# A later block's seventh mask one pair of tiles sooner, the weights' low parts in other heads, GELU's table loaded behind the last exponential

## The chip, the cores and the metric

The kernel runs on one core of one Trainium2 chip. The metric is the device time of one execution in microseconds (us); less is better.

## The reference

One layer of attention over a graph with 2048 nodes, 256 features and 8 heads of 32, in float32. The source side is normed twice (a layer norm and a rectifier, then the layer's own norm), the target side once. Logits are masked by an adjacency matrix of integers before the softmax. Projection, second norm, a feed-forward part with 1024 hidden features and sums follow.

```python
h = maximum(layernorm(x), 0)
hs, ht = layer_norm(h, g1, b1), layer_norm(h_target, g1, b1)
q = (ht @ Wq + bq).reshape(T, 8, 32) / sqrt(32)
k, v = (hs @ Wk + bk), (hs @ Wv + bv)            # in heads
logits = where(adj != 0, einsum('thd,shd->hts', q, k), -1e30)
ctx = einsum('hts,shd->thd', softmax(logits), v).reshape(T, 256)
ht = layer_norm(ht + ctx @ Wo + bo, g2, b2)
out = x + ht + gelu(ht @ W1) @ W2                # tanh form of gelu
```

## The kernel before

**Tiling.** The targets are cut into 4 blocks of 512. A unit is one block and one head, so there are 32 units; unit u has block k = u // 8 and place r = u % 8 in the block. A unit has 16 steps, one for each tile of 128 sources, and 8 pair indices j, one for two steps.

**One step.** TensorE makes the scores of step n + 5 in one of two banks (`scores`: four products that put in the mask and one of keys and queries), ScalarE takes the exponential of them into one of 8 slots of `prob` (`exponential`, L945), and the float32 result is used as two 16-bit parts: the high one is read in place, the low one is a subtraction (`low_part`). VectorE makes the low parts of the steps in `DVE_LO` (2, 6, 10 and 14 of most units, L1324), GpSimd the other twelve (L1532). TensorE then multiplies both parts with the values (`context`). At the end of a unit ScalarE reads the context (`context_out`, L967).

**Row maxima.** The exponential needs a shift for each row. TensorE therefore makes the scores of a unit already some 14 pairs ahead, as `early` products of 128 targets by 1024 sources, in two banks of two halves each, one half in each step. VectorE subtracts the mask and takes the maximum of each (`maxima`, L1316). The early product e waits for the maxima of e - 2, as it writes the same bank. In unit u, pair index j handles e = 8u + 14 + j.

**Masks.** For the next block the adjacency of 512 by 2048 is loaded in eight pieces of 128 by 1024 (512 KB each) into two buffers `adj_in`, and turned into a mask. ScalarE makes pieces 0 and 7, VectorE pieces 1 to 6 at the places (r, j) of `MASK_DVE` (`make_mask`, L1304). In VectorE's program one pair index has this order:

```python
            if k + 1 < NTB and (r, s - 3) in QP_AT:
                query_low(k + 1, QP_AT[r, s - 3])
        for n in lo_here(u, j):
            low_part(n)
        for e in pairs_at(u, j):
            maxima(e)
        ...
        if k + 1 < NTB and (r, j) in MASK_DVE:
            make_mask(k + 1, MASK_DVE[r, j])
```

SyncE issues all loads and copies in one queue: for a block the pieces of the mask, at r = 4 the last two of them, then the 12 copies of the next block's queries (`place_q`) behind the query low part.

**Other work in the loop**, at fixed places (r, s): transposes of targets, queries and contexts on TensorE through one bank `aux`, norms on ScalarE, statistics (`lead_stats` at r = 3, j = 3 to 6) on VectorE, low parts of features on GpSimd. At (4, 1) of blocks 1 to 3 ScalarE takes a square root and so loads a table and, for the next exponential, loads another.

**Weights.** `W1` and `W2` are also used in two 16-bit parts. ScalarE makes the eight high parts at s = 6 of the units in `HIGH_AT` = 3, 4, 5, 6, 7, 12, 13, 14 (`weight_high`), GpSimd the eight low parts (`weight_low`, L1578) behind step 12 of the units in `LOW_AT`. All are read after the loop, but for the first four low parts, on which the normed features of block 0 wait in unit 29.

**After the loop** come the feed-forward products: `up_products` in groups of 6 matmuls, `gelus` on ScalarE (L1189), then the high part (L1193), the low part on VectorE, `down_products`. A product of index f waits for the GELU of f - 2.

The engines run their programs in order; waits are semaphores, and each change of order is one of the program text. Table loads of ScalarE are put by the compiler ahead of the first activation that needs another table.

Of the kernel before, what the change touches and what calls it, by code (L numbers as in the profile page):

```python
# [10 lines left out]
ACT = mybir.ActivationFunctionType  # L11
# [51 lines left out]
HT_AT = {(5, 1): 0, (5, 4): 1}  # L63


MASK_DVE = {(2, 3): 1, (2, 6): 2, (3, 2): 3, (3, 7): 4, (4, 3): 5, (4, 7): 6}


MASK_ACT = {0: [(0, 2), (0, 4), (0, 11), (0, 13)], 7: [(5, 13), (5, 15), (6, 1), (6, 3)]}
# [22 lines left out]


HIGH_AT = [3, 4, 5, 6, 7, 12, 13, 14]
LOW_AT = [4, 5, 6, 7, 13, 14, 15, 21]


DVE_LO = [(10, 14)] + [(4, 9, 14) if u == UNITS - 3 else (2, 6, 10, 14) for u in range(1, UNITS - 2)] + [tuple(range(1, STEPS, 2))] * 2
# [2 lines left out]
def head_of(r):  # L101

    return r % 2 * TT + r // 2
# [71 lines left out]
def masks_dve(k, i):  # L175

    return min(i + 1, FIRST_DVE) if k == 0 else len(MASK_DVE) * (k - 1) + FIRST_DVE + min(i, len(MASK_DVE))

# [16 lines left out]
def gnn_kernel(nc, x, adj, nodemask, h_target, ln1_scale, ln1_bias, Wq, bq, Wk, bk, Wv, bv, Wo, bo,  # L195
               ln2_scale, ln2_bias, W1, W2, out):
    with ExitStack() as top:
# [6 lines left out]
        def sem(name):  # L204
            return top.enter_context(nc.semaphore(name))
# [49 lines left out]
        big_c, eps_c, warm_c = (big[:, i:i + 1] for i in range(3))  # L255
# [58 lines left out]
        dve_link, act_link, pool_link = sem("dve_link"), sem("act_link"), sem("pool_link")  # L314
# [62 lines left out]
        def raw_of(k):  # L377
            return raw[:, k % 2, :].rearrange("p (t h w) -> p t h w", t=TT, h=H)
# [21 lines left out]
        with nc.Block() as block:  # L400
# [464 lines left out]
            def _(act):  # L865
# [7 lines left out]
                def affine(dst, tile, scale, bias):  # L873
                    return nc.scalar.activation(dst, tile, ACT.Identity, bias=bias, scale=scale)
# [62 lines left out]
                def exponential(n):  # L937
                    act.wait_ge(score_ready, n + 1)
                    if n >= SLOTS:
                        act.wait_ge(ctx_done, n - SLOTS + 1)  # L940
                    elif n == 0:

                        act.wait_ge(mask_dve, FIRST_DVE)
                        act.wait_ge(mask_pool, PAIRS - FIRST_DVE)
                    nc.scalar.activation(prob[:, n % SLOTS, :], score[n % 2][:, :], ACT.Exp).then_inc(exp_done, 1)  # L945
# [14 lines left out]
                def row_out(u):  # L960
                    job_here("shift", u)
                    nc.scalar.activation(q_block(u // H)[SHIFT_ROW:SHIFT_ROW + 1, u % H, :], aux[SHIFT_ROW:SHIFT_ROW + 1, :],
                                         ACT.Copy).then_inc(aux_done, 1)

                def context_out(u):
                    act.wait_ge(ctx_done, (u + 1) * STEPS)
                    nc.scalar.activation(raw_of(u // H)[:, :, head_of(u % H), :], ctx_v, ACT.Copy).then_inc(ctx_out, 1)  # L967
# [107 lines left out]
                def normed_high(k, c, bank):  # L1075
                    if k > 0:

                        act.wait_ge(h_lo, DC * (k - 1) + c + 1)
                    else:
                        act.wait_ge(w_lo, 4)  # L1080
                    read, count = (h_done, DC * (k - 1) + c + 1) if k > 0 else (aux_done, AUX["hT", 0, c] + 1)
                    affine(h_full[:, c, :], bank, LN2_G[:, c:c + 1], LN2_B[:, c:c + 1]).then_inc(read, 1)
                    act.wait_ge(read, count)
                    nc.scalar.activation(h_bufs[k % 2][:, 0, c, :], h_full[:, c, :], ACT.Copy).then_inc(h_hi, 1)
# [44 lines left out]
                for u in range(UNITS):  # L1129
                    k, r = divmod(u, H)  # L1130
                    for s in range(STEPS):
                        n = u * STEPS + s
                        if s == 0 and u > 0:
                            context_out(u - 1)
                        if n + AHEAD < TILES:
                            exponential(n + AHEAD)
                        job = aux_job(u, s + 2)
                        if job == ("shift", u + 1):
                            negated(u + 1)
                        if aux_job(u, s - 1) == ("shift", u + 1):  # L1140
                            row_out(u + 1)
                        if k == 0 and (r, s) in T_HIGH[0]:
                            feature_high(0, T_HIGH[0].index((r, s)))
                        if k + 1 < NTB and (r, s) in T_HIGH[1]:
                            feature_high(k + 1, T_HIGH[1].index((r, s)))
                        if (u, s) == WO_HIGH:
                            output_high()
                        if s == 6 and u in HIGH_AT:
                            weight_high(HIGH_AT.index(u))
                        if k + 1 < NTB:  # L1150
                            if act_mask_at(k, r, s):
                                i, part = act_mask_at(k, r, s)
                                mask_part(k + 1, i, part)
                            if r == 2 and s in TARGET_STEPS:
                                target_norm(k + 1, TARGET_STEPS.index(s))
                            if (r, s - 1) in QT_AT:
                                query_features(k + 1, QT_AT[r, s - 1])
                            if (r, s - 2) in QP_AT:
                                if QP_AT[r, s - 2] == 0:
                                    for g in range(TT):  # L1160
                                        act.wait_ge(q_placed[g], PLACE * (k + 1))
                                query_high(k + 1, QP_AT[r, s - 2])
                        if k > 0:
                            for part in range(NORM_STEPS):
                                if (r, s - part) in NORM_AT:
                                    context_norm(k - 1, NORM_AT.index((r, s - part)), part)
                            if (r, s - 1) in CT_AT:
                                context_T(k - 1, CT_AT[r, s - 1])
                            if (r, s - 2) in CT_AT:
                                context_high(k - 1, CT_AT[r, s - 2])  # L1170
                            if (r, s - 2) in WO_AT:
                                rows_out(k - 1, WO_AT[r, s - 2])
                            if r == 4 and s == 1:
                                row_deviation(k - 1, lead_width(k - 1))
                            if r == 5 and s in (2, 4, 7, 11):
                                second_norm(k - 1, (2, 4, 7, 11).index(s))
                        if k == NTB - 1:
                            if (r, s - 1) in HT_AT:
                                job_here("hT", 0, HT_AT[r, s - 1])
                                normed_high(0, HT_AT[r, s - 1], aux[:, :])  # L1180
                context_out(UNITS - 1)


# [40 lines left out]
            def _(dve):  # L1224
# [207 lines left out]
                for u in range(UNITS):  # L1432
                    k, r = divmod(u, H)
                    for j in range(PAIRS):
# [9 lines left out]
                        if u == 0 and j in (4, 5):  # L1444
                            target_norm(j - 3)
                        if k + 1 < NTB and (r, j) in MASK_DVE:
                            make_mask(k + 1, MASK_DVE[r, j])
                        if k > 0:
# [73 lines left out]
            def _(pool):  # L1522
# [51 lines left out]
                def weight_low(i):  # L1574
                    pool.wait_ge(w_hi, i + 1)
                    lo, w, hi = (a.rearrange("p c n -> p (c n)")[:, i % 4 * TB:(i % 4 + 1) * TB]
                                 for a in ((w1_lo, w1, w1_hi) if i < 4 else (w2_lo, w2, w2_hi)))
                    nc.gpsimd.tensor_tensor(lo, w, hi, ALU.subtract).then_inc(w_lo, 1)  # L1578
# [44 lines left out]
                for u in range(UNITS):  # L1623
                    k, r = divmod(u, H)
                    for m in range(STEPS):
                        if m not in DVE_LO[u]:
                            low_part(u * STEPS + m)
                        if k > 0 and (r, m) == LEAD_SCALE:
                            lead_scale(k - 1, lead_width(k - 1))
                        if k > 0 and (r, m) in SUM_AT:  # L1630
                            context_sum(k - 1, SUM_AT.index((r, m)))
                        if k == 0 and (r, m) in T_LOW[0]:
                            feature_low(0, T_LOW[0].index((r, m)))
                        if k + 1 < NTB and (r, m) in T_LOW[1]:
                            feature_low(k + 1, T_LOW[1].index((r, m)))
                        if k > 0 and (r, m) in C_LOW:
                            context_low(k - 1, C_LOW.index((r, m)))
                        if (u, m) == WO_LOW:
                            output_low()
                        if m == 12 and u in LOW_AT:  # L1640
                            weight_low(LOW_AT.index(u))

                for t in range(TT):
                    context_sum(NTB - 1, t)
# [39 lines left out]
```

## Time and profile before

| | us |
|---|---|
| median of 3 runs | 683.53 |
| the runs | 681.89, 683.53, 683.69 |
| the profiled execution's own time | 682.28 |
| its span | 680.3 |
| TensorE busy | 649.9 |
| VectorE busy | 567.2 |
| GpSimd busy | 542.4 |
| ScalarE busy | 501.5 |

The span runs from the first to the last instruction in the profile. Matmuls are pipelined and their ends are modelled: one of 512 columns has a duration of 0.38 us, and the next one starts 0.22 us behind its start. So idle time of TensorE under about 0.15 us doesn't show as such. The granted clock of TensorE was 1.00 in every stage of the loop. The names in the rows are those of the tensors; where two share memory, the older name may stand (`nTq`, `qT` and `kT` in the rows of the feed-forward part, `w_f` for the 16-bit weights).

### The profile page before, as it was taken

What the parts mean: (1) busy time and instruction counts of PE and PEld (TensorE: products, weight loads), DVE (VectorE), ACT (ScalarE), POOL (GpSimd) and SP (SyncE); (2) the same over time, 40 slices, a digit from 0 to 9 for tenths busy, and PEclk for the clock granted to TensorE, in tenths of its full rate; (3) what the DMA queues carried; (4) which work ended last, traced back from release to release, by engine and by line L of the source; (5) the groups of instructions that cost most, each with busy time, mean ns of one, the idle gap of its engine ahead of it and who ended that gap; (6) DMA issues with size and microseconds to landing.
All of it is one profiled execution on the core that took longest, in us unless ns stands there. A gap on an engine that the chain in (4) does not pass through costs nothing. (4 is left out here: it accounts for less than half of the span.)

```text
span 680.3 us, 20543 instructions
## 1 busy us (share of the span) xinstructions
PE 649.9 (96%) x8402; PEld 464.2 (68%) x8402; DVE 567.2 (83%) x940; ACT 501.5 (74%) x973; POOL 542.4 (80%) x508
## 2 busy tenths in 40 slices
PE   4999999999999999999999999999999999899998
PEld 4556677766777777677777766777777667457767
DVE  5989899999989979888988798899878887595561
ACT  4767687777789858787898686877976788877450
POOL 4565889999999967999999679999997777383430
PEclk9999999999999999999999999999999999999999
DMA  8835512212101011220011112011000000000001
GB/s 290 281 91 151 167 33 64 64 50 63 33 2 34 2 65 63 67 76 2 2 33 33 64 55 57 19 67 59 4 2 1 2 2 2 1 1 32 24 18 54
DMA packets 20797, 36.23 MB, mean 53 GB/s; under 512 B 2752, under 2 KB 13280, under 8 KB 20704
## 3 DMA queue, kind: packets, MB, share of 16 engines
q1 hardware_dynamic: 20704, 34.92, 16.5%
q8 instruction: 66, 1.08, 0.7%
q14 instruction: 27, 0.22, 0.1%
HBM read 26.49 MB, written 2.10 MB: 42 GB/s over the span
## 5 line engine op out<-in xcount | busy, mean ns | idle before, releaser
L1532 POOL TENSOR_TENSOR prob_lo<-prob 128x512 f16<-128x512 f32 x379 | 432.5, 1168 | 45.7 <-ACT prob L945 44.7
L945 ACT ACTIVATE prob<-score 128x512 f32<-128x512 f32 x512 | 303.8, 597 | 110.4 <-PE score L514 102.5
L514 PE MATMUL score<-nidentb,mask_nat 128*128 128x128 bf16 x2048 | 198.3, 219 | 4.2 <-ACT prob L945 1.6
L514 PEld LDWEIGHTS ctx<-v_sb,prob 128*128 128x128 bf16 x2048 | 158.8, 98 | 61.9 <-ACT raw L967 13.8
L514 PE MATMUL early<-kT,qT 96*128 96x512 f16 x512 | 191.8, 380 | 6.7 <-DVE half_max L1316 5.7
L514 PE MATMUL score<-qT,kT 97*128 97x512 f16 x512 | 195.3, 381 | 0.0
L514 PE MATMUL ctx<-v_sb,prob 128*128 128x65 f16 x2048 | 191.5, 193 | 2.9 <-ACT raw L967 2.5
L1316 DVE CUSTOM_DVE_ANT_0 early<-early,mask_nat,half_max 128x1024 f32<-128x1024 f32 x128 | 163.9, 1286 | 33.3 <-PE early L514 31.7
L514 PE MATMUL ctx<-v_sb,prob_lo 128*128 128x65 f16 x2048 | 190.4, 193 | 0.0
L514 PEld LDWEIGHTS ctx<-v_sb,prob_lo 128*128 128x128 f16 x2048 | 142.6, 97 | 49.7 <-issue 4.0
L1316 DVE CUSTOM_DVE_ANT_0 early<-early,mask_nat 128x1024 f32<-128x1024 f32 x128 | 157.0, 1229 | 19.3 <-PE early L514 16.6
L1324 DVE TENSOR_TENSOR prob_lo<-prob 128x512 f16<-128x512 f32 x133 | 133.7, 1006 | 4.1 <-ACT prob L945 4.0
L514 PEld LDWEIGHTS score<-nidentb,mask_nat 128*128 128x128 bf16 x2048 | 121.5, 97 | 9.9 <-ACT prob L945 4.3
L514 PEld LDWEIGHTS early<-kT,qT 96*128 96x128 f16 x512 | 50.3, 99 | 17.5 <-DVE half_max L1316 13.3
L514 PEld LDWEIGHTS score<-qT,kT 97*128 97x128 f16 x512 | 50.1, 98 | 0.0
L514 PE MATMUL early<-w_f,kT 128*128 128x256 f16 x384 | 42.8, 273 | 1.1 <-DVE adj_in L1484 1.1
L1461 DVE TENSOR_TENSOR kT<-qT,kT 128x512 f16<-128x512 f32 x32 | 28.0, 885 | 17.7 <-ACT kT L1193 17.5
L514 PEld LDWEIGHTS early<-w_f,kT 128*128 128x128 f16 x384 | 37.4, 98 | 6.6 <-DVE adj_in L1484 1.7
L1660 POOL TENSOR_TENSOR mask_nat<-mask_nat,tgt 128x256 f32<-128x256 f32 x16 | 16.5, 1039 | 27.4 <-DVE mask_nat L1475 27.4
L1316 DVE DVE_READ_ACCUMULATOR2_ANT half_max<- 128x1 f32 x256 | 35.4, 138 | 0.0
L1189 ACT ACTIVATE qT<-score 128x512 f32<-128x512 f32 x32 | 19.0, 592 | 17.0 <-PE score L514 12.2
L983 ACT ACTIVATE q_stage<-raw,rden 128x32 f32<-128x32 f32 x96 | 25.3, 316 | 0.2
(185 smaller groups left out, 650.7 us busy)
## 6 DMA issues: line engine op xcount, KB each, us to landing
adj_in<-in_adj SPq DMA_DIRECT2D x26, 512.0 KB, 3.9
qT<-q_stage SPq DMA_DIRECT2D x48, 64.0 KB, 2.0
kT<-mask_nat SPq DMA_DIRECT2D x48, 64.0 KB, 2.0
raw<-in_x SPq DMA_DIRECT2D x4, 512.0 KB, 5.4
tgt<-in_L_gnn_h_target SPq DMA_DIRECT2D x4, 512.0 KB, 11.3
prob<-in_adj SPq DMA_DIRECT2D x4, 512.0 KB, 10.1
nT<-in_L_gnn_W SPq DMA_DIRECT2D x2, 1024.0 KB, 6.2
mask_nat<-in_x SPq DMA_DIRECT2D x1, 2048.0 KB, 9.7
```

What stands on the lines that cost most here:

```text
L514: return nc.tensor.matmul(dst, w, m, start=start, stop=stop, **more)
L945: nc.scalar.activation(prob[:, n % SLOTS, :], score[n % 2][:, :], ACT.Exp).then_inc(exp_done, 1)
L983: last = nc.scalar.activation(cnorm[:, t, h * HD:(h + 1) * HD], raw_of(k)[:, t, h, 0:HD], ACT.Copy, scale=rden[:, t * H + h:t * H + h + 1])
L1189: nc.scalar.activation(gelu[:, f % 2, :], up[f % 2][:, :], ACT.Gelu_apprx_tanh).then_inc(gelu_ready, 1)
L1316: nc.vector.tensor_tensor_reduce(out=early[e % 2][:, :], in0=early[e % 2][:, :], in1=mask_nat[:, k % 2, t, half * HALF:(half + 1) * HALF], ...
L1324: nc.vector.tensor_tensor(prob_lo[:, n % SLOTS, :], prob[:, n % SLOTS, :], prob_hi(n % SLOTS), ALU.subtract).then_inc(lo_sem["dve"], 1)
L1461: nc.vector.tensor_tensor(g_lo[:, k % 2, f, :], gelu[:, f % 2, :], g_hi[:, k % 2, f, :], ALU.subtract).then_inc(g_lo_done, 1)
L1532: nc.gpsimd.tensor_tensor(prob_lo[:, n % SLOTS, :], prob[:, n % SLOTS, :], prob_hi(n % SLOTS), ALU.subtract).then_inc(lo_sem["pool"], 1)
L1660: nc.gpsimd.tensor_tensor(xin[:, n - 1, :], xin[:, n - 1, :], tgt[:, n - 1, :], ALU.add).then_inc(r_done, 1)
```

## The change

Three edits. The seventh mask (piece 6) of the blocks 1 to 3 is made at pair index 6 of the unit with r = 4, where it was index 7. The eight low parts of weights stand behind other steps: three in unit 11, three in unit 19 and two in unit 20, where it was one each in eight units. And ScalarE runs a one-column GELU on a constant behind the loop and ahead of the last `context_out`, so that the table is loaded there.

```diff
-MASK_DVE = {(2, 3): 1, (2, 6): 2, (3, 2): 3, (3, 7): 4, (4, 3): 5, (4, 7): 6}
+MASK_DVE = {(2, 3): 1, (2, 6): 2, (3, 2): 3, (3, 7): 4, (4, 3): 5, (4, 6): 6}
...
-LOW_AT = [4, 5, 6, 7, 13, 14, 15, 21]
+LOW_AT = [(11, 3), (11, 8), (11, 13), (19, 3), (19, 8), (19, 13), (20, 2), (20, 7)]
...
+
+                nc.scalar.activation(warm_c, eps_c, ACT.Gelu_apprx_tanh).then_inc(act_link, 1)
                 context_out(UNITS - 1)
...
-                        if m == 12 and u in LOW_AT:
-                            weight_low(LOW_AT.index(u))
+                        if (u, m) in LOW_AT:
+                            weight_low(LOW_AT.index((u, m)))
```

## Rows read from the trace of the kernel before

**Rows 1.** The page, part 1: busy us, share of the span, instructions.

```profile
PE 649.9 (96%) x8402; PEld 464.2 (68%) x8402; DVE 567.2 (83%) x940; ACT 501.5 (74%) x973; POOL 542.4 (80%) x508
```

**Rows 2.** The waits of TensorE, 90 to 575 us: total, times, longest.

```profile
PE early L514 <- DVE half_max L1316: 4.3, 9, 0.9
```

**Rows 3.** Windows of three units: length, then busy us (instructions) of each engine.

```profile
149.06:165.34 16.28, 15.57 (x230) 10.74 (x229) 15.78 (x23) 11.85 (x22) 16.28 (x14) 1.00 0.31 83
165.34:180.40 15.06, 14.89 (x229) 10.91 (x229) 12.65 (x20) 12.02 (x23) 15.06 (x15) 1.00 0.12 37
245.38:263.07 17.69, 17.51 (x257) 13.50 (x257) 14.40 (x29) 12.08 (x23) 12.92 (x13) 1.00 0.17 54
```

**Rows 4.** The lines of two operations: duration in ns, least/median/most.

```profile
L1304 DVE TENSOR_SCALAR mask_nat<-adj_in x20: 676/825/1504, 33.8 to 414.9; 128x1024 bf16<-128x1024 int32 x20
...
L1324 DVE TENSOR_TENSOR prob_lo<-prob x133: 677/954/1566, 74.1 to 580.1; 128x512 f16<-128x512 f32 x133
...
L1532 POOL TENSOR_TENSOR prob_lo<-prob x379: 1031/1040/1577, 63.8 to 579.4; 128x512 f16<-128x512 f32 x190
```

**Rows 5.** The page, part 6: one kind of DMA issue, us to landing.

```profile
adj_in<-in_adj SPq DMA_DIRECT2D x26, 512.0 KB, 3.9
```

**Rows 6.** VectorE in order of time: start, duration, [idle before].

```profile
146.60 1.29 DVE L1316 CUSTOM_DVE_ANT_0 early<-early,mask_nat,half_max 128x1024 f32<-128x1024 f32 x1 [0.78 <-PE early L514]
...
148.47 0.71 DVE L1324 TENSOR_TENSOR prob_lo<-prob 128x512 f16<-128x512 f32 x1
149.10 1.28 DVE L1316 CUSTOM_DVE_ANT_0 early<-early,mask_nat,half_max 128x1024 f32<-128x1024 f32 x1
...
150.31 1.32 DVE L1304 TENSOR_SCALAR mask_nat<-adj_in 128x1024 bf16<-128x1024 int32 x1
...
154.00 1.28 DVE L1316 CUSTOM_DVE_ANT_0 early<-early,mask_nat,half_max 128x1024 f32<-128x1024 f32 x1
```

**Rows 7.** TensorE in order of time, two early matmuls.

```profile
150.83 0.38 PE L514 MATMUL early<-kT,qT 96*128 96x512 f16 x1
...
155.39 0.39 PE L514 MATMUL early<-kT,qT 96*128 96x512 f16 x1 [0.47 <-DVE half_max L1316]
```

**Rows 8.** GpSimd in order of time, the first low part of the weights.

```profile
142.91 1.16 POOL L1578 TENSOR_TENSOR w_f<-nT,w_f 128x512 f16<-128x512 f32 x1
```

**Rows 9.** VectorE in order of time, unit 11.

```profile
253.33 0.69 DVE L1304 TENSOR_SCALAR mask_nat<-adj_in 128x1024 bf16<-128x1024 int32 x1
...
258.84 0.76 DVE L1324 TENSOR_TENSOR prob_lo<-prob 128x512 f16<-128x512 f32 x1
259.51 1.22 DVE L1316 CUSTOM_DVE_ANT_0 early<-early,mask_nat 128x1024 f32<-128x1024 f32 x1
```

**Rows 10.** GpSimd in order of time, unit 11 and, last, unit 20.

```profile
250.69 2.04 POOL L1532 TENSOR_TENSOR prob_lo<-prob 128x512 f16<-128x512 f32 x2 [0.74 <-ACT prob L945]
...
258.00 3.48 POOL L1532 TENSOR_TENSOR prob_lo<-prob 128x512 f16<-128x512 f32 x3 [0.64 <-ACT prob L945]
...
399.97 3.04 POOL L1532 TENSOR_TENSOR prob_lo<-prob 128x512 f16<-128x512 f32 x3 [2.85 <-ACT prob L945]
```

**Rows 11.** TensorE in order of time, one early matmul.

```profile
260.96 0.38 PE L514 MATMUL early<-kT,qT 96*128 96x512 f16 x1
```

**Rows 12.** ScalarE in order of time, at the end of the attention.

```profile
573.28 6.76 ACT L945 ACTIVATE prob<-score 128x512 f32<-128x512 f32 x10 [0.43 <-PE score L514]
581.94 0.39 ACT L967 ACTIVATE raw<-ctx 128x260 f32<-128x260 f32 x1 [1.90 <-PE ctx L514]
582.35 1.28 ACT L1189 ACT_TABLE_LOAD   x1
583.64 0.60 ACT L1189 ACTIVATE qT<-score 128x512 f32<-128x512 f32 x1
...
588.00 0.60 ACT L1189 ACTIVATE qT<-score 128x512 f32<-128x512 f32 x1 [0.79 <-PE score L514]
```

**Rows 13.** TensorE in order of time, the first up products.

```profile
581.74 4.05 PE L514 MATMUL score<-nTq,w_f 128*128 128x512 f16 x18
```

## The prediction

> **What bounds the kernel now.** I read the page first: TensorE is busy 649.9 of 680.3 us and the other three engines 501.5 to 567.2 [rows 1]. So a change pays only where TensorE stands still or is held up, and it costs only where it makes TensorE stand. Then I read who makes TensorE wait between 90 and 575 us, the attention loop without its fill: the longest entry is 4.3 us in nine waits for the row maxima of VectorE (`half_max`, L1316) [rows 2]. The other entries name ScalarE, none names GpSimd. Then I read the windows of single units (one head of one target block, 16 steps). An undisturbed unit takes 15.06 us; the unit behind the one whose end carries the seventh mask (149.06 to 165.34, the sixth unit of the first block) takes 16.28, though it has no more matmuls (230 against 229) [rows 3]. This 1.2 us is the stall that the first edit is near to, and the same pattern comes once in each of the three blocks that have a next one. GpSimd is busy for the whole of these two units, but for only 12.92 of 17.69 us of the first unit that gets new work [rows 3].
>
> One more view carries the argument: how long one and the same instruction takes. A low part on VectorE takes 677 to 1566 ns, a mask 676 to 1504 ns, a low part on GpSimd 1031 to 1577 ns [rows 4]. The shapes are equal. In the order of time the short VectorE durations stand where GpSimd is idle or just between two instructions, the long ones where a GpSimd instruction has just begun. So an instruction of VectorE with both ends in SBUF waits for the running one of GpSimd, up to 1566 - 677 = 0.89 us, and GpSimd's next one pays about half a microsecond (up to 1577 ns for 1040). The maxima (1.22 to 1.29 us) read PSUM and stay put. Work that moves on GpSimd therefore has a price on VectorE, and VectorE is what TensorE waits for. The Trainium skill has this as a rule ("SBUF — State Buffer", the diagram's notes: the pair of ports that VectorE and GpSimd share is an exclusive lock, held for a whole instruction, and the other one blocks fully). The trace agrees in direction; its longest delay of VectorE, 0.89, is under the 1.04 us of one GpSimd instruction that the rule allows, and by the rule the upper bounds below would each be 0.15 higher.
>
> **The mask a pair sooner.** The seventh mask of blocks 1 to 3 goes from behind `maxima` of pair index 7 of the fifth unit to behind that of index 6. Counts and waits are unchanged, as it is still the sixth of its block on VectorE. Its input was loaded into `adj_in` when the fifth mask was made, about a unit earlier, and lands in 3.9 us [rows 5], so no new wait. In the first block VectorE is idle for 0.78 us before the maxima at 146.60 and from there without a gap until behind 155 us [rows 6]. The mask stays behind those maxima, so it doesn't go into the gap. What was maxima, query low part, low part, maxima, mask, maxima becomes maxima, mask, query low part, low part, maxima, maxima: the same instructions, the same sum, the same end. What changes is what lies between: the second of these maxima (149.10 + 1.28 = 150.38) ends about 1.24 us later (1.32 less the overlap of neighbours), at 151.6. The early matmul that needs it ran at 150.83 [rows 7]: a new stall of about 151.7 - 150.8 = 0.9 us. The matmul at 155.39 waited for the maxima that end at 154.00 + 1.28 = 155.28 [rows 6, 7], which don't move, so the old stalls behind (0.47 of idle at 155.39 [rows 7] and smaller ones that the modelled ends of matmuls hide; 1.2 in all by the units' lengths) shrink by as much as the new one costs. Net 0 in each of three blocks. The low part for step 2 of the next unit (148.47 + 0.71 = 149.18 [rows 6]) ends some 1.3 us later, about 150.5, and its context product comes at about 151.1 or later: hidden. The query low part also ends 1.3 us later, and with it SyncE issues 12 copies of queries (`place_q`); their first reader is more than a unit later, so hidden, and the next block's first load behind them in the same queue has a whole unit too. Bound: the mask and the low part land on another phase of GpSimd, at worst 0.8 us either way, per block; three draws together, plus or minus 1.0. I take 0.
>
> **The weights' low parts.** Eight instructions of GpSimd of 1.16 us [rows 8], in units 4, 5, 6, 7, 13, 14, 15, 21 before, are now three each in units 11 and 19 and two in unit 20 (counted from 0). Their inputs, the high parts, are made in units 3 to 14 and each stands ahead of its low part; their readers (the normed features of unit 29 and the products after the loop) come later. Units 11 and 19 have r = 3: GpSimd has 17.69 - 12.92 = 4.8 us free there, 3 x 1.16 = 3.5 fits [rows 3]. The context products don't wait for it.
>
> But where it fits in, it meets VectorE. In unit 11 GpSimd works off two low parts at 250.69 to 252.73, VectorE's mask at 253.33 runs behind them in 0.69 us, and before 258.00 it is idle for 0.64, so VectorE's low part at 258.84 takes 0.76 [rows 9, 10]. The new instruction behind step 8 moves the second of the pair to about 252.8 to 253.8: the mask waits some 0.3 us more. The one behind step 13 ends at about 258.7, the low part of step 15 then runs to about 259.7, and VectorE's low part, begun at 259.1, ends at about 260.3 in place of 259.6: 0.7 us later in all. The maxima behind it end at 259.51 + 1.22 = 260.73 now [rows 9], and 261.43 then; the early matmul that reads them came at 260.96 [rows 11]. A waiting matmul starts 0.11 behind the end of its maxima (155.39 against 155.28 [rows 6, 7]), so TensorE stands 261.43 + 0.11 - 260.96 = 0.57 us. It is not given back: the next point at which VectorE holds TensorE lies behind idle time of VectorE, so it starts from TensorE's own delay. Unit 19 has the same order: 0.57 again. Bounds for each: 0 if the phases miss, and 2 x 0.89 - 0.12 = 1.7 if both instructions pay in full.
>
> Unit 20 has ScalarE's two table loads, in which GpSimd is idle for 2.85 us [rows 10]; the first of its two new instructions, 1.16 us, shifts work into that idle time, in which VectorE now has a mask and a low part for itself, at the short end of their durations [rows 4]; the second pushes the rest of the unit by 1.15. VectorE has about a microsecond there before TensorE asks, half of it just won by the stall of unit 19. I take +0.2, between 0 and 0.9.
>
> What the eight leave: GpSimd's run behind the first, from 144.07 on [rows 8], starts 1.15 us sooner. It frees no wait that TensorE has today [rows 2], only other phases for the two shared instructions that end in the stall of unit 5. I take -0.3, between -1.2 (the whole stall) and +0.5. In units 6, 7, 13 to 15 and 21 nothing waits: 0.
>
> **GELU's table.** Today the load of 1.28 us starts at 582.35 behind `context_out`, and the first GELU runs at 583.64; the change loads it behind the last exponential (573.28 + 6.76 = 580.04), in the 1.90 us in which ScalarE waits for the last context product: 580.05 to 581.33, and the small activation 0.2, so 0.4 before 581.94 [rows 12]. Free. The gain is none as well: TensorE runs the first three groups of the up projection as 18 matmuls in one piece of 4.05 us from 581.74 and is not held by the first GELU; by 588.00 ScalarE itself has waited 0.79 us for TensorE, and everything behind hangs on that point [rows 12, 13]. 0; if the cover were gone, `context_out` would be late by at most the 1.28, and even that comes back in the first GELU. The Trainium skill ("ScalarE: Activation LUTs", What ACT_TABLE_LOAD costs) gives 1283 ns and a drain of about 1380 more for a switch. The load is 1.28 here, but the activation follows at once (582.35 + 1.28 = 583.63 against 583.64). By the page `context_out` would be about 1.0 late and the sum still unchanged.
>
> **Sum.** 2 x 0.57 + 0.2 - 0.3 + 0 + 0 = +1.0 us. On the profiled execution's own 682.28 us (its span is 680.3, with 2.0 around it) that is 683.3; that execution lies 1.25 below the median of the runs, 683.53, so the forecast for the median is 684.5.
>
> **Rivals.**
> (1) All is hidden: the new instructions meet VectorE in other phases than today's rows say, about 0. For it: only the 0.23 us between 260.73 and 260.96 decide, and they are read off one execution. Against it: GpSimd's order fixes the phase. 683.5.
> (2) The mask's move does dissolve the stall of unit 5, 13 and 21: up to 1.2 us in each, 3.6 in all, 679.9. This needs VectorE to have idle time ahead of the mask's new place that it lacks at the old one, or GpSimd to stand still there. Against it: no gap on VectorE from 146.60 to 155. Half of it, 1.8, would be 681.7.
> (3) The load of GELU's table was on the path: 1.3 less, 682.2. Against it: the unbroken 18 matmuls.
> (4) Slower: VectorE pays in full for GpSimd's new work. At 1.7 in unit 11 and in unit 19 and 0.9 in unit 20 it is 4.3 less 0.3, 687.5; it passes 0.3% when the mask and the low part in units 11 and 19 lose together 1.0 or more each, against 0.7 in my working. For it: GpSimd's new instructions stand where it is idle today [rows 10].
>
> **How the numbers follow.** A measurement of this kernel can tell about 0.3% (2.05 us) from no change. Chances: my forecast (+0.3 to +2.0) 0.50; (1) 0.27; (2) 0.08, of which half passes 0.3%; (3) 0.04; (4) 0.11. Faster by over 0.3%: 0.05; within: 0.84; slower: 0.11. The range 682.0 to 686.3 takes in (1), (3) nearly, the near half of (4) and the spread of the three runs (1.8 us); the rest of (2) and (4) is outside.
>
> **What would show it.** After: the mask row directly behind the maxima of index 6, an early matmul in step 2 of units 5, 13 and 21 that waits 0.8 to 0.9 us for `half_max`, and less waiting in steps 4 and 6; those units still about 16.3 us long. In units 11 and 19 the mask near 1.0 and the low part of step 14 near 1.1 us, with an early matmul waiting about 0.5 at the unit's end, and the two units with their followers about 0.6 us longer than now. ScalarE: table load at 580.05, first GELU about 0.4 earlier, the fourth unchanged against TensorE. I am wrong if units 5, 13 and 21 get shorter by 0.5 or more each, or if VectorE's instructions in unit 11 keep 0.69 and 0.76.

## The result, and the profile after

The changed kernel takes 684.07 us (median of 14 runs, 683.83 to 685.64) against 682.03 (median of 14 runs, 681.77 to 683.69): 2.04 us more. The ratio is 1.0031, with a 95% interval of 1.0024 to 1.0038, so it is slower, by about the 0.3% that the prediction took as the least that can be told from no change. The time lies in the range on record; the forecast of +1.0 us was half of what came.

The page of the changed kernel; the span is 2.2 us longer, and no engine has more to do than before but ScalarE, with its one added activation [rows 1].

```profile
span 682.5 us, 20544 instructions
...
PE 649.2 (95%) x8402; PEld 463.0 (68%) x8402; DVE 566.0 (83%) x940; ACT 501.8 (74%) x974; POOL 540.5 (79%) x508
```

The waits of TensorE in its attention loop, 90 to 575 us. The maxima now cost 5.9 us in nine waits, where it was 4.3 [rows 2], and GpSimd has its first entry in this list:

```profile
PE early L514 <- DVE half_max L1318: 5.9, 9, 1.1
...
PE ctx L514 <- POOL prob_lo L1534: 0.2, 1, 0.2
```

Windows of units 5, 6 and 11 (length, busy us of TensorE, its weight loads, VectorE, ScalarE, GpSimd). A unit u is taken from the start of the exponential of step 16u + 5 to that of the next unit. Unit 5 has hardly changed [rows 3]; unit 11 takes 18.42 us for 17.69:

```profile
149.12:165.45 16.33, 15.24 (x230) 10.90 (x229) 15.00 (x24) 11.75 (x23) 14.71 (x13) 1.00 0.31 83
165.45:180.51 15.06, 14.89 (x229) 10.91 (x230) 12.17 (x20) 12.02 (x24) 13.44 (x14) 1.00 0.11 37
245.60:264.02 18.42, 17.74 (x257) 13.35 (x258) 15.23 (x28) 12.10 (x24) 16.88 (x16) 1.00 0.16 51
```

Unit 19 is the same as 11. All lengths that changed, from the starts of these exponentials in each trace (us):

| unit | before | changed | mask only | weights only | mask at index 5 | weights at 3, 4, 5 | weights at 3, 4, 13 | weights at 1, 3, 4 | last version |
|---|---|---|---|---|---|---|---|---|---|
| 5 | 16.28 | 16.33 | 16.43 | 17.14 | 15.98 | 16.32 | 16.31 | 16.32 | 15.35 |
| 7 | 14.90 | 15.08 | 14.90 | 15.07 | 14.90 | 15.07 | 15.08 | 15.08 | 14.90 |
| 11 | 17.70 | 18.41 | 17.70 | 18.40 | 17.70 | 18.59 | 18.03 | 17.69 | 17.69 |
| 13 | 16.25 | 16.40 | 16.39 | 16.25 | 15.40 | 16.40 | 16.40 | 16.39 | 15.40 |
| 15 | 14.90 | 15.08 | 14.90 | 15.08 | 14.90 | 15.08 | 15.08 | 15.07 | 14.90 |
| 19 | 17.69 | 18.41 | 17.70 | 18.41 | 17.69 | 18.59 | 18.03 | 18.59 | 17.69 |
| 20 | 18.72 | 18.77 | 18.72 | 18.76 | 18.72 | 18.71 | 18.77 | 18.72 | 18.73 |
| 21 | 16.39 | 16.62 | 16.55 | 16.44 | 15.55 | 16.42 | 16.62 | 16.41 | 15.56 |

The others stay within 0.1 us, but for unit 28 in the profiles of two kernels (last section). In these rows "changed" less "before" adds up to 2.27 us, and units 10 and 16 give back 0.06 and 0.09: 2.12. Two thirds of it, 1.43, are in units 11 and 19.

**Unit 11.** GpSimd, VectorE and TensorE of the changed kernel in order of time, each in a fence of its own:

```profile
251.91 1.16 POOL L1580 TENSOR_TENSOR w_f<-nT,w_f 128x512 f16<-128x512 f32 x1
...
257.93 1.16 POOL L1580 TENSOR_TENSOR w_f<-nT,w_f 128x512 f16<-128x512 f32 x1
```

```profile
253.56 1.07 DVE L1306 TENSOR_SCALAR mask_nat<-adj_in 128x1024 bf16<-128x1024 int32 x1
...
259.44 1.19 DVE L1326 TENSOR_TENSOR prob_lo<-prob 128x512 f16<-128x512 f32 x1
260.56 1.22 DVE L1318 CUSTOM_DVE_ANT_0 early<-early,mask_nat 128x1024 f32<-128x1024 f32 x1
```

```profile
261.89 0.39 PE L514 MATMUL early<-kT,qT 96*128 96x512 f16 x1 [0.35 <-DVE half_max L1318]
```

The answering rows of before are [rows 9 to 11]. The mask, 0.69 us then, waits for GpSimd's low part behind the new instruction at 251.91 and takes 1.07; the low part, 0.76 then, meets GpSimd's low part behind the new instruction at 257.93 and takes 1.19. The maxima end at 260.56 + 1.22 = 261.78, the early matmul that was issued at 260.96 starts at 261.89, 0.11 behind that end, as worked out. (0.22 of its lateness is from further ahead: unit 11 starts at 245.60 for 245.38.)

**Units 4 and 5.** VectorE, and the early matmul of step 2:

```profile
146.66 1.29 DVE L1318 CUSTOM_DVE_ANT_0 early<-early,mask_nat,half_max 128x1024 f32<-128x1024 f32 x1 [0.89 <-PE early L514]
...
147.87 1.26 DVE L1306 TENSOR_SCALAR mask_nat<-adj_in 128x1024 bf16<-128x1024 int32 x1
...
149.71 0.86 DVE L1326 TENSOR_TENSOR prob_lo<-prob 128x512 f16<-128x512 f32 x1
150.50 1.28 DVE L1318 CUSTOM_DVE_ANT_0 early<-early,mask_nat,half_max 128x1024 f32<-128x1024 f32 x1
...
153.94 1.28 DVE L1318 CUSTOM_DVE_ANT_0 early<-early,mask_nat,half_max 128x1024 f32<-128x1024 f32 x1
```

```profile
151.89 0.39 PE L514 MATMUL early<-kT,qT 96*128 96x512 f16 x1 [1.00 <-DVE half_max L1318]
```

The mask stands behind the maxima at 146.66. The maxima that this matmul needs end at 151.78 for 150.38, and TensorE stands 1.00 us; in return the maxima at 153.94 are over in time, and the wait that stood at 155.39 [rows 7] is gone.

**Unit 7,** where GpSimd has less to do than before, is 0.18 us longer. The waits of TensorE's weight loads, 179.51 to 196.59 us (before, no wait for `half_max` stood there); then GpSimd and VectorE in order of time:

```profile
PEld early L514 <- DVE half_max L1318: 0.5, 2, 0.3
```

```profile
182.99 3.48 POOL L1534 TENSOR_TENSOR prob_lo<-prob 128x512 f16<-128x512 f32 x3 [0.24 <-ACT prob L945]
```

```profile
183.18 1.40 DVE L1326 TENSOR_TENSOR prob_lo<-prob 128x512 f16<-128x512 f32 x1
```

Before, the same low part of VectorE took 1.06:

```profile
182.87 1.06 DVE L1324 TENSOR_TENSOR prob_lo<-prob 128x512 f16<-128x512 f32 x1
```

GpSimd has caught up: it waits for the exponential, starts right behind it, and VectorE's low part begins 0.19 us later and takes 0.72 more than the 0.68 that it takes alone. The next one of the unit goes from 0.95 to 1.37 in the same way.

**The end of the attention,** ScalarE:

```profile
582.24 1.28 ACT L1182 ACT_TABLE_LOAD   x1
583.53 0.20 ACT L1182 ACTIVATE big<-big 128x1 f32<-128x1 f32 x1
584.13 0.39 ACT L967 ACTIVATE raw<-ctx 128x260 f32<-128x260 f32 x1 [0.40 <-PE ctx L514]
585.43 0.60 ACT L1191 ACTIVATE qT<-score 128x512 f32<-128x512 f32 x1 [0.91 <-PE score L514]
...
590.19 0.60 ACT L1191 ACTIVATE qT<-score 128x512 f32<-128x512 f32 x1 [0.88 <-PE score L514]
```

The table load is hidden and `context_out` is not late for it: it waited 0.40 us for TensorE. The small activation follows 0.01 us behind the end of the load, so nothing like the later `context_out` that the prediction worked out from a drain is seen. The fourth GELU (590.19) is 2.19 us behind its time of before, 588.00 [rows 12], which is what was lost up to unit 21. Nothing is gained.

### The profile page after: what moved, and what is told of

It reads as the page before. It is cut to its first block and busy times, and to the rows that moved or that the text cites. A ratio compares the mean times of both kernels' runs of the same rounds, so it can differ in the third digit from the quotient of the medians.

```text
span 682.5 us, 20544 instructions
## 1 busy us (share of the span) xinstructions
PE 649.2 (95%) x8402; PEld 463.0 (68%) x8402; DVE 566.0 (83%) x940; ACT 501.8 (74%) x974; POOL 540.5 (79%) x508
## 3 DMA queue, kind: packets, MB, share of 16 engines
q8 instruction: 66, 1.08, 0.6%
## 5 line engine op out<-in xcount | busy, mean ns | idle before, releaser
L1326 DVE TENSOR_TENSOR prob_lo<-prob 128x512 f16<-128x512 f32 x133 | 129.8, 977 | 4.0 <-ACT prob L945 4.0
```

The lines of the kernel that those rows point to most:

```text
L1326: nc.vector.tensor_tensor(prob_lo[:, n % SLOTS, :], prob[:, n % SLOTS, :], prob_hi(n % SLOTS), ALU.subtract).then_inc(lo_sem["dve"], 1)
```

## The experiments

The theories: (A) the loss is VectorE's two-sided SBUF instructions meeting GpSimd's new work in units 11, 19 and 20; (B) it is the new stall of 1 us in units 5, 13 and 21; (D) VectorE's gapless stretch makes the stall of these units, and the mask would fit into the gap ahead of it.

**The three edits one by one,** and the mask one pair further.

```diff
# mask alone: the first hunk of the change; weights alone: the second and the last; GELU alone: the third
# mask at pair index 5, on the kernel before:
-MASK_DVE = {..., (4, 3): 5, (4, 7): 6}
+MASK_DVE = {..., (4, 3): 5, (4, 5): 6}
```

> The kernel before with the mask's edit alone. Theory A (the loss comes from GpSimd's new work in units 11, 19 and 20, which VectorE's instructions wait for; the mask's move only moves a stall): units 5, 13 and 21 within 0.2 us of the kernel before each, the whole +0.1 to +0.5 us (ratio 1.0002 to 1.0007). Rival B (the stall of 1.0 us in step 2 that shows in units 5, 13 and 21 of the changed kernel is the loss): about +1.5 us or more, ratio 1.002 or over.

> The kernel before with the low parts of the weights at their new steps alone. Theory A: +1.5 to +2.0 us, ratio 1.0022 to 1.0029, with units 11 and 19 at 18.4 us for 17.7. Rival B: under +0.7 us.

> The kernel before with the GELU ahead of the last context read alone. Both theories: 0, within 0.2 us. A third, that the table load was on the path, says -1.3 us (ratio 0.998).

> The kernel before with the seventh mask two pairs sooner, at pair index 5 of the fifth unit. Theory D (VectorE's gapless stretch behind the maxima at 146.60 makes the stall of the next unit, and the idle 0.8, 1.8 and 1.7 us ahead of those maxima can hold the mask): the stall of units 5, 13 and 21 goes, these units fall from 16.3 to about 15.3 us, the whole -2 to -3.3 us (ratio 0.995 to 0.997). Rival (the stall is not made by the mask, or the mask there makes the maxima late by as much): 0 within 0.5 us.

| kernel | median us (runs) | before, us | ratio, 95% interval |
|---|---|---|---|
| mask alone | 682.71 (11) | 682.15 | 1.0010, 1.0001 to 1.0018 |
| weights alone | 684.75 (5) | 682.15 | 1.0042, 1.0030 to 1.0055 |
| GELU alone | 682.01 (11) | 682.15 | 1.0001, 0.9992 to 1.0010 |
| mask at index 5 | 680.18 (7) | 682.15 | 0.9974, 0.9963 to 0.9985 |

The mask alone costs 0.56 us, hardly more than the 0.5 that I expected of it at most, the GELU nothing, and the weights 2.6: theory B falls. A is right on units 11 and 19, but too low as a whole (1.5 to 2.0 expected), for it had no loss in unit 5. The edits don't add up: 0.56 + 2.6 - 0.14 = 3.0 against 2.04. The table shows the place: unit 5 takes 17.14 us with the weights alone and 16.33 with the mask moved too. VectorE there, with the weights alone:

```profile
148.30 1.58 DVE L1324 TENSOR_TENSOR prob_lo<-prob 128x512 f16<-128x512 f32 x1
149.81 1.28 DVE L1316 CUSTOM_DVE_ANT_0 early<-early,mask_nat,half_max 128x1024 f32<-128x1024 f32 x1
...
151.01 1.32 DVE L1304 TENSOR_SCALAR mask_nat<-adj_in 128x1024 bf16<-128x1024 int32 x1
```

The low part takes 1.58 us for 0.71 [rows 6]. It begins at 148.30, the moment in which GpSimd, now one instruction earlier in its queue, begins one too, and waits for nearly all of it: 0.87 of 1.04. With the mask ahead of it, as in the changed kernel, it begins later and takes 0.86. So it is luck of phase, and the relief that I had put down as a gain of 0.3 was a loss of 0.86 by itself.

The gap in the second block, in the kernel before:

```profile
279.52 1.29 DVE L1316 CUSTOM_DVE_ANT_0 early<-early,mask_nat,half_max 128x1024 f32<-128x1024 f32 x1 [1.83 <-PE early L514]
```

The mask at index 5 there:

```profile
277.02 1.50 DVE L1304 TENSOR_SCALAR mask_nat<-adj_in 128x1024 bf16<-128x1024 int32 x1
278.98 1.29 DVE L1316 CUSTOM_DVE_ANT_0 early<-early,mask_nat,half_max 128x1024 f32<-128x1024 f32 x1 [0.45 <-PE early L514]
...
280.85 1.11 DVE L1324 TENSOR_TENSOR prob_lo<-prob 128x512 f16<-128x512 f32 x1
...
283.09 0.14 DVE L1316 DVE_READ_ACCUMULATOR2_ANT half_max<- 128x1 f32 x1
```

It lies in the gap of 1.8 us ahead of the maxima, of which 0.45 stay, though it meets GpSimd and takes 1.50. Units 13 and 21 are 0.85 us shorter each. Unit 5 gains 0.30 only, and unit 4 loses 0.08. Its maxima are over in time too (no wait for `half_max` is left there); what stands now is TensorE behind GpSimd's low part, in the waits of 140 to 170 us (the wait, then us in total, times, the longest):

```profile
PEld ctx L514 <- POOL prob_lo L1532: 2.2, 5, 0.8
```

In the kernel before the same row has 0.7 us in two waits: GpSimd has no idle time in units 4 and 5, and its queue is the next bound there as soon as VectorE's is out of the way.

The whole is -2.0, at the near end of what I had expected; D holds, and its first block was overrated.

**The weights' places, and one of them alone.** The last one is on the kernel before, with its old mask and GELU.

```diff
# on the changed kernel, units 11 and 19 (x):
-(x, 3), (x, 8), (x, 13)
+(x, 3), (x, 4), (x, 5)        # then: (x, 3), (x, 4), (x, 13), then: (x, 1), (x, 3), (x, 4)
# the first with the mask at index 5 too: "all mended"
# on the kernel before, the first low part alone:
-(4, 12), ...
+(3, 12), ...
```

> The changed kernel with the three low parts of weights in units 11 and 19 behind steps 3, 4 and 5 in place of 3, 8 and 13: the same work of GpSimd in the same units, away from VectorE's gapless stretch. Theory A (it is the meeting of single instructions): units 11 and 19 fall from 18.4 to 17.7 to 17.95 us, where 0.3 us on the mask may stay, as GpSimd is behind until about 253.8; the whole 682.7 to 683.2 us. Rival (it is the amount of GpSimd's work in these units): units 11 and 19 stay at 18.3 to 18.5.

> The changed kernel with the low parts of weights in units 11 and 19 behind steps 3, 4 and 13. Theory A: the mask behind index 2 is back to 0.69 us, the low part of step 14 still takes about 1.15, and units 11 and 19 are at 17.95 to 18.15 us. Rival (amount of work): 18.4.

> The changed kernel with the mask at pair index 5 and the low parts of weights behind steps 3, 4, 5. Theory A and D: units 13 and 21 at 15.4 to 15.6, unit 5 at 15.4 to 16.0, units 11 and 19 at 17.7 to 17.95, units 7 and 15 at 15.08; the whole -1.2 to -2.2 us against the kernel before (ratio 0.997 to 0.998). Rival (the gains don't stand together, as mask and weights did not): above -0.5.

> The kernel before with the first low part of the weights alone moved, from step 12 of unit 4 to step 12 of unit 3, where GpSimd has 1.7 us idle. GpSimd's run in units 4 and 5 is then one instruction of 1.16 us shorter. Theory A (phases): VectorE's low part at the start of unit 5 meets GpSimd's instruction at its beginning and takes about 1.58 us for 0.71, as with all weights moved, and unit 5 takes 17.1 us for 16.3. Rival (less work of GpSimd ahead is never worse): 16.3 or less.

> The changed kernel with the three low parts of weights in units 11 and 19 behind steps 1, 3 and 4, where GpSimd stands idle for 2.0 and 1.8 us and has caught up before the mask behind index 2. Theory A (it is the meeting of single instructions): the mask stays at 0.69 and the low part of step 14 near 0.76 us, units 11 and 19 are at 17.7 us, the whole about 682.7 us (ratio to the kernel before 1.001). Rival (the amount of GpSimd's work in these units): 18.0 or more in each.

| kernel | median us (runs) | before, us | ratio, 95% interval |
|---|---|---|---|
| weights at 3, 4, 5 | 684.47 (8) | 682.25 | 1.0031, 1.0021 to 1.0041 |
| weights at 3, 4, 13 | 683.45 (1) | 682.25 | one run, no interval |
| all mended | 681.75 (11) | 682.25 | 0.9993, 0.9984 to 1.0002 |
| first low part in unit 3 | 683.30 (1) | 682.25 | one run, no interval |
| weights at 1, 3, 4 | 683.24 (10) | 682.07 | 1.0019, 1.0010 to 1.0028 |

Steps 3, 4, 5 are a miss: I expected 17.7 to 17.95 us for unit 11 and it takes 18.59. The queue of GpSimd is behind until 253.7, the mask waits 0.46 us, and VectorE is later by about as much for the rest of the unit. Its low part at 259.08 begins 0.30 behind the start of GpSimd's, though no weight is near it any more, and takes 1.28:

```profile
253.11 1.15 DVE L1306 TENSOR_SCALAR mask_nat<-adj_in 128x1024 bf16<-128x1024 int32 x1
...
259.08 1.28 DVE L1326 TENSOR_TENSOR prob_lo<-prob 128x512 f16<-128x512 f32 x1
```

With steps 3, 4, 13 the mask is clear, and only the low part pays, 1.20; the unit takes 18.03, within what A gave:

```profile
253.48 0.69 DVE L1306 TENSOR_SCALAR mask_nat<-adj_in 128x1024 bf16<-128x1024 int32 x1
...
258.99 1.20 DVE L1326 TENSOR_TENSOR prob_lo<-prob 128x512 f16<-128x512 f32 x1
```

With steps 1, 3, 4 unit 11 takes 17.69, that of the kernel before, with the same three instructions in it. That settles it against the amount of work as the cause: the same three instructions cost 0, 0.33, 0.71 or 0.89 us by their places. Unit 19, with the same steps, takes 18.59 for the 17.7 that I expected, and so the whole 683.24 for 682.7. Unit 10 had a stall of TensorE of 0.94 us and takes 19.22 us, unit 18 takes 18.11, so, as I read it, GpSimd has more time to catch up ahead of unit 11: its first moved instruction starts 1.13 us ahead of the mask there (241.87 against 243.00) and 0.07 behind it ahead of unit 19. There it is held up by the mask, holds up VectorE's low part, and GpSimd has no gap until 389.7. GpSimd, then VectorE:

```profile
375.07 1.63 POOL L1580 TENSOR_TENSOR w_f<-nT,w_f 128x512 f16<-128x512 f32 x1
376.67 1.48 POOL L1534 TENSOR_TENSOR prob_lo<-prob 128x512 f16<-128x512 f32 x1
...
381.80 7.92 POOL L1534 TENSOR_TENSOR prob_lo<-prob 128x512 f16<-128x512 f32 x7
```

```profile
375.00 0.69 DVE L1306 TENSOR_SCALAR mask_nat<-adj_in 128x1024 bf16<-128x1024 int32 x1
375.60 1.65 DVE L1326 TENSOR_TENSOR prob_lo<-prob 128x512 f16<-128x512 f32 x1
...
385.37 1.01 DVE L1306 TENSOR_SCALAR mask_nat<-adj_in 128x1024 bf16<-128x1024 int32 x1
...
391.19 1.43 DVE L1326 TENSOR_TENSOR prob_lo<-prob 128x512 f16<-128x512 f32 x1
```

The low part waits for the weight and takes 1.65, and GpSimd doesn't catch up before the mask at 385.37, which takes 1.01 (0.69 in unit 11), and the low part at 391.19, which takes 1.43.

With the first low part in unit 3 the one run of the kernel is 1.0 us slower: unit 4 takes 19.11 us for 18.50, unit 5 16.65 for 16.28 and unit 8 0.10 more. I had expected a loss in unit 5 alone. The 0.6 of unit 4 comes from work put ahead of it, not from work taken away: GpSimd had 1.7 us idle in unit 3 as a whole, but only 0.23 behind step 12. So its queue enters unit 4 1.1 us late (129.59 for 128.45), and TensorE waits for it:

```profile
131.22 0.19 PE L514 MATMUL ctx<-v_sb,prob 128*128 128x65 f16 x1 [0.45 <-POOL prob_lo L1532]
```

In unit 5 I expected 1.58 us for the low part; it is 1.08:

```profile
149.11 1.08 DVE L1324 TENSOR_TENSOR prob_lo<-prob 128x512 f16<-128x512 f32 x1
150.11 1.28 DVE L1316 CUSTOM_DVE_ANT_0 early<-early,mask_nat,half_max 128x1024 f32<-128x1024 f32 x1
```

The direction stands in unit 5, the exact phase wasn't to be foretold; and as unit 4 changed with it, this run doesn't isolate the relief. The weights alone do, where unit 4 keeps its 18.50 us. "All mended" takes 0.5 us less than before, where I expected 1.2 to 2.2, and its interval doesn't tell it from nothing, for its weights lie at 3, 4, 5: units 5, 13 and 21 give 0.94, 0.85 and 0.69, and units 11 and 19 take 0.9 each back.

**A version that beats both.**

```diff
# on the kernel before, with its old GELU
-MASK_DVE = {..., (4, 7): 6}
+MASK_DVE = {..., (4, 5): 6}
-LOW_AT = [4, 5, 6, 7, 13, 14, 15, 21]
+LOW_AT = [(11, 1), (11, 3), (6, 12), (7, 12), (13, 12), (14, 12), (15, 12), (21, 12)]
```

> A version that should beat both kernels: the mask at pair index 5, the first two low parts of the weights behind steps 1 and 3 of unit 11, the other six where they were (step 12 of units 6, 7, 13, 14, 15, 21), no early GELU. Theory A and D: unit 5 at 15.3 to 15.5, units 13 and 21 at 15.4 to 15.6, units 7 and 15 at 14.9, units 11 and 19 at 17.7; the whole -2.4 to -2.9 us (ratio 0.9958 to 0.9965). If the gain in unit 5 does not come with only these two gone, -2.0.

It is the mask in the gap, and the low parts of the weights that stood in units 4 and 5 put at steps 1 and 3 of unit 11. 679.57 us (median of 5 runs) against 682.07: ratio 0.9962, interval 0.9950 to 0.9975, 2.5 us less and within the 2.4 to 2.9 expected. Unit 5 now has the full gain, 15.35 us for 16.28, and the wait for GpSimd is down to one of 0.2 us (as it is in "all mended", where these two low parts are gone from units 4 and 5 as well; one of 0.4 us for `half_max` is back in both), in the same view and stretch:

```profile
PEld ctx L514 <- POOL prob_lo L1532: 0.2, 1, 0.2
```

Units 13 and 21 stay at 15.40 and 15.56, 11 and 19 at 17.69. It is 4.5 us faster than the changed kernel. The window of unit 5:

```profile
149.10:164.45 15.35, 15.11 (x230) 10.77 (x227) 14.49 (x22) 11.74 (x23) 14.91 (x14) 1.00 0.33 88
```

## Why the prediction was half right

The price of the two units with three new instructions was right; the price of what was taken away was not. That 684.5 came within 0.4 us of 684.07 is luck: it stands on a median of three runs, 683.53, which lies 1.5 above the 682.03 of fourteen, and this makes up for more than the 1.0 that the forecast of the change was short. The change itself, +2.04, lies just above my +0.3 to +2.0, to which I gave half of the chances, and on the line of 0.3%, beyond which I gave 0.11.

- **What bounds.** Right for this change: the large losses show as TensorE waiting for `half_max`, and the price of GpSimd's work was paid on VectorE. Not the whole of it: with the mask at index 5 that wait is gone from unit 5, and GpSimd's queue bounds it.
- **Weights in units 11 and 19.** Right in place and mechanism; 0.57 expected, 0.71 and 0.72 measured. The mask lost 0.38 for my 0.3 and the low part 0.43 for my 0.4. Part of TensorE's wait came at an early matmul sooner, at 257.33 for 256.80, which the prediction didn't have. Rival (4) asked for 1.0 or more lost on the two together; it was 0.81, and what brought the loss to 0.3% lies in other units.
- **Unit 20.** 0.2 expected; with the weights alone units 20 and 21 lose 0.04 and 0.05. The 0.28 that both lose in the changed kernel holds 0.16 of the mask's move, in unit 21.
- **What the eight leave.** The step that failed is "I take -0.3" for unit 4 and "in units 6, 7, 13 to 15 and 21 nothing waits: 0". Alone it was +0.86 in unit 5 and 0.17 and 0.18 in units 7 and 15, where TensorE had no wait for `half_max` before. A GpSimd that has caught up starts each low part right behind its exponential, just ahead of VectorE's, as in the rows of unit 7. Less work ahead was worse in all three. In the changed kernel unit 5 lost only 0.05, for the mask stood ahead of the low part, which then took 0.86.
- **The mask.** 0 expected, +0.15, +0.14 and +0.16 measured alone. The swap of one stall for another was as described (1.00 against 0.9 for the new one), but the units got some 0.15 longer all the same; I had equated the new stall and the old ones, though nothing makes the new one end where the last of the old did.
- **GELU.** Right, 0, for the reasons given.
- **Rival (2)** named the right condition, idle time of VectorE ahead of the mask's new place; index 6 doesn't have it, and index 5, one pair further ahead, does.

By the rows of before, the terms that I could price by a row (0.57) came within a quarter. Of the 1.1 us by which the units' lengths, 2.12, pass the forecast, 0.3 are in units 11 and 19; nearly all the rest, some 0.85 less the 0.15 that units 10 and 16 give back, is in units 5, 7, 13 and 15, whose terms I set at zero or below for want of a wait: a phase has no row. What stays open is the 0.15 us per block between the old stalls and the new one.

## What to carry to other kernels

Where the instructions of two engines hold each other up, place one by the idle time of both engines, read in order of time, and not by the free share of a stretch: the same three instructions cost 0 to 0.9 us by their steps. Look in the waiting engine's row for the gap ahead of the stretch that is late, and put the movable work there. And don't book relief of an engine that nobody waits for as a gain: it shifts the phases of the others, and here that alone lost up to 0.9 us; the same relief gave 0.6 us of unit 5 once the wait ahead of it was gone.

## What the runs showed of the hardware that was not expected

The profiled executions of two kernels (mask alone and GELU alone) show something that the others don't: in unit 28, for 3.4 us, TensorE's granted clock is 0.50 of full speed, the lower of its two levels (1.2 GHz of 2.4), and unit 28 takes 18.60 and 18.52 us for 17.00. Windows around it in the profile of the mask alone; the last columns are granted clock, DMA share and GB/s:

```profile
526.00:530.70 4.70, 2.94 (x45) 1.89 (x41) 4.70 (x7) 4.34 (x7) 1.79 (x2) 1.00 0.02 3
530.70:534.10 3.40, 3.38 (x28) 2.29 (x29) 0.49 (x3) 1.64 (x3) 3.03 (x3) 0.50 0.00 0
534.10:540.00 5.90, 5.90 (x96) 4.42 (x93) 5.10 (x11) 4.07 (x9) 4.14 (x6) 1.00 0.01 1
```

TensorE was busy for 2.94 of the 4.7 us ahead of it, while ScalarE loaded the table for the square root and then that of the exponential. In the profile of the kernel before it was busy for 2.94 of the same 4.7 us too, and the clock stays at 1.00, as in those of all the other kernels. So the same idle time brings the fall in some executions and not in others. Of the 11 runs of the mask alone, two have a mean granted clock of 0.997, and they take 684.09 and 684.34 us where the median is 682.71.

An instruction on VectorE takes up to 1.65 us for 0.68 (weights at 1, 3, 4), 0.97 more: nearly as long as one GpSimd instruction, 1.04, or 1.16 for one of the weights. That is nearer than the 0.89 read before to the rule of the Trainium skill ("SBUF — State Buffer", the diagram's notes), by which the ports that the two engines share are locked for a whole instruction. By this rule the bound of 1.7 us for two instructions would be 0.3 higher, and not 0.15 as the prediction has it. GpSimd's next instruction starts at 376.67, 0.58 us ahead of the end of VectorE's (375.60 + 1.65 = 377.25), and takes 1.48 us for 1.04: it loses 0.45 us.
